# Local attention of a decoder: where the queries' reciprocal norms are applied, which engine guards them, and the order of the set-up

## The reference, cut to what matters

```python
q, k, v = split(h @ wqkv)                  # 8 heads of 64
q = q / max(norm(q), 1e-12) * q_scale
k = k / max(norm(k), 1e-12) * k_scale
q, k = rotary_xpos(q, k)                   # t * cos * s + rotate_half(t) * sin * s
sim = where(mask, -max, (q * 8) @ k.T)     # each window of 64 tokens and the one before
x = x + (softmax(sim) @ v) @ wo
```

## Time and profile before

| | |
|---|---|
| median of three runs | 3974.55 us |
| the profiled execution, its own time | 3975.32 us |
| its span in the profile | 3973.6 us |
| granted TensorE clock, mean | 0.986 |
| busy share of the span: TensorE, VectorE, ScalarE, GpSimd | 95%, 73%, 72%, 46% |
| layer 0 of local attention | about 1100 to 1640 us of the span |
| layer 1 | about 1801 to 2340 us |
| eight exponentials (L1168) | 312.0 us busy in 1024 operations, mean 389 ns |

### The profile page before, as it was taken

The page is one execution under the profiler, slowest core; times in us unless marked ns, Lnnn a source line. Parts: engine busy times, 40 slices in busy tenths (PEclk is TensorE's granted clock), DMA queues, the critical chain, the costliest instruction groups (busy, mean ns, idle before and its releaser), DMA issues. The chain is left out here.

```text
span 3973.6 us, 108219 instructions
## 1 busy us (share of the span) xinstructions
PE 3761.6 (95%) x35018; PEld 3030.0 (76%) x35018; DVE 2920.3 (73%) x7397; ACT 2875.6 (72%) x6740; POOL 1823.0 (46%) x1666
## 2 busy tenths in 40 slices
PE   8999899999979999897999989999999989998998
PEld 6777688888746666685666668788888877776888
DVE  7888655555579999656999965676777768886665
ACT  5555466656579999856999975677777768886665
POOL 5555322222268888635777764333333332111222
PEclk9999999999999999999999999999999999999999
DMA  1000100000100000100000010000000000000444
GB/s 30 19 20 19 53 7 7 6 6 6 41 11 8 8 8 8 24 22 9 9 8 8 9 25 20 17 0 0 0 0 0 0 1 4 3 4 25 126 121 116
DMA packets 130766, 80.29 MB, mean 20 GB/s; under 512 B 95328, under 2 KB 121184, under 8 KB 130016
## 3 DMA queue, kind: packets, MB, share of 16 engines
q1 hardware_dynamic: 130656, 78.87, 7.5%
HBM read 57.39 MB, written 4.72 MB: 16 GB/s over the span
## 5 line engine op out<-in xcount | busy, mean ns | idle before, releaser
L1101 POOL TENSOR_TENSOR l_rc<-l_rc,l_rs 128x1024 f32<-128x1024 f32 x128 | 303.6, 2372 | 201.8 <-DVE l_rs L1293 201.8
L1168 ACT ACTIVATE l_prob<-l_prob,l_mx 128x128 f32<-128x128 f32 x1024 | 312.0, 389 | 0.0
L672 POOL TENSOR_TENSOR ca_prob<-ca_prob,ca_sm 128x1232 f32<-128x1232 f32 x64 | 143.9, 2249 | 307.5 <-DVE ca_sm L835 307.5
L1779 POOL TENSOR_TENSOR mb_steps<-w_upto,mb_dta 128x1024 f32<-128x1024 f32 x64 | 121.4, 1897 | 345.8 <-DVE mb_dta L2047 345.8
L1193 PE MATMUL l_qk_ps<-w_local,l_hT 128*128 128x512 f32 x512 | 248.9, 610 | 12.5 <-DVE l_rs L1293 9.3
L1095 POOL TENSOR_TENSOR l_prob<-l_prob,l_sm 128x1024 f32<-128x1024 f32 x128 | 242.8, 1897 | 16.9 <-DVE l_sm L1279 16.9
L1078 POOL TENSOR_TENSOR l_rc<-l_rc,l_ss 128x1024 f32<-128x1024 f32 x128 | 243.4, 1902 | 12.4 <-POOL l_rc L1101 4.5
L1938 PE MATMUL mb_x_ps<-w_wx,mb_xT 128*128 128x256 f32 x1024 | 237.1, 385 | 0.0
L382 ACT ACTIVATE la_ef<-la_feat,la_fbias 128x1024 f32<-128x1024 f32 x128 | 135.6, 1110 | 122.2 <-PE la_feat L441 122.2
L346 POOL TENSOR_SCALAR la_ef<-la_ef,la_high,la_low 128x1024 f32<-128x1024 f32 x128 | 151.1, 1190 | 135.0 <-ACT la_ef L382 135.0
L1288 DVE TENSOR_REDUCE l_ss<-l_sq 128x16 f32<-128x1024 f32 x128 | 156.1, 1219 | 77.3 <-ACT l_sq L1132 76.5
(11 more groups left out here) (348 smaller groups left out, 11788.6 us busy)
## 6 DMA issues: line engine op xcount, KB each, us to landing
mo_spread<-parked SPq DMA_DIRECT2D x128, 256.0 KB
la_xin<-in_x SPq DMA_DIRECT2D x64, 64.0 KB
la_xT<-in_x_T SPq DMA_DIRECT2D x64, 64.0 KB, 1.8
l_h<-lt_y SPq DMA_DIRECT2D x128, 32.0 KB
lt_quad<-lt_y SPq DMA_DIRECT2D x32, 128.0 KB
out_x<-k_x SPq DMA_DIRECT2D x64, 64.0 KB, 1.6
l_h<-lt_y SPq DMA_DIRECT2D x128, 31.8 KB
lt_quad<-lt_y SPq DMA_DIRECT2D x32, 127.0 KB
```

The costliest lines, as they stand in the source:

```text
L1101: gp.tensor_tensor(wide(rc[l][:]), wide(rc[l][:]), wide(rs[l][:]), ALU.add).then_inc(*pool_sum.did("rot"))
L1168: ex = sc.activation(p[:, a, j], p[:, a, j], ACT.Exp, bias=mx[l][:, a, j:j + 1])
```

## The change

The norms of k are still applied to k, on GpSimd, but as a multiply of 512 elements. Those of q are no longer applied to q: they become the `scale` operand of the eight exponentials, one column of `ss` for each head, and the bias becomes the negated maximum times the reciprocal norm, `shift`, computed on GpSimd (128x8). `ss` has four buffers for that instead of two. The guard against zero is a maximum with 1e-24 on GpSimd instead of a Relu on ScalarE, and the Ln has no bias any more. The tables are laid out so that both sine products are one VectorE operation that doesn't swap halves; the swap moves into GpSimd's add, which becomes two operations of 512 elements, in runs of 32. TensorE's transposes of q wait for that add alone, those of k for the multiply. On ScalarE hT now comes ahead of the exponentials as before, then four exponentials, then Ln and Exp on `ss` (of batch n-3), then the other four. The quad rows are cleared after the other engines have been let go.

```diff
@@ set-up, semaphores
-        under, floor = m.sb("under", [128, 1]), m.sb("floor", [128, 1])
+        floor = m.sb("floor", [128, 2 * H])
-        ss = both(m, "ss", [T, 3, 2 * H])
+        ss = [m.sb(f"ss{i}", [T, 3, 2 * H]) for i in range(4)]
-        NZERO = 10
+        NZERO = 5
@@ sync
                 pipeline(sp, g.NB, OUT + 1, step, turn=4)
+                sp.wait_ge(cleared, 4)
@@ gpsimd
-                for slot in range(4):
-                    gp.memset(g.quads[slot][0:1], 0.0).then_inc(zeroed, 1)
-                gp.memset(under[:], -1e-24).then_inc(zeroed, 1)
-                gp.memset(floor[:], 1e-24 * 2.0 ** 20).then_inc(zeroed, 1)
+                gp.memset(floor[:], 1e-24).then_inc(zeroed, 1)
+                gp.wait_ge(zeroed, NZERO)
...
+                for slot in range(4):
+                    gp.memset(g.quads[slot][0:1], 0.0).then_inc(cleared, 1)
...
                     b = at(SCORE)
-                        gp.wait_ge(*pool_sum.at("rot", b))
                         gp.wait_ge(*act_rot.at("rn", b))
-                        gp.tensor_tensor(rc[l][:].rearrange("p a h e -> p (a h) e"), rc[l][:].rearrange("p a h e -> p (a h) e"),
-                                         ss[l][:, 2].unsqueeze(2).to_broadcast([T, 2 * H, HD]), ALU.mult
-                                         ).then_inc(*pool_norm.did("norm"))
+                        gp.wait_ge(*pool_sum.at("rot1", b))
+                        gp.tensor_tensor(rc[l][:, 1], rc[l][:, 1], ss[b.slot][:, 2, H:2 * H].unsqueeze(2).to_broadcast([T, H, HD]),
+                                         ALU.mult).then_inc(*pool_norm.did("norm"))
+                    b = at(SOFT)
+                        gp.wait_ge(*vec_max.at("max", b))
+                        gp.wait_ge(*act_exp.at("exp", b, ago=2))
+                        gp.tensor_tensor(shift[l][:], mx[l][:], ss[b.slot][:, 2, 0:H].rearrange("p (j a) -> p a j", a=2),
+                                         ALU.mult).then_inc(*pool_shift.did("shift"))
...
                     b = at(QKV)
-                        gp.wait_ge(*vec_rot.at("sin1", b))
-                        gp.tensor_tensor(wide(rc[l][:]), wide(rc[l][:]), wide(rs[l][:]), ALU.add
-                                         ).then_inc(*pool_sum.did("rot"))
+                        gp.wait_ge(*vec_rot.at("ss", b))
+                        gp.sem_inc(turns, 1)
+                        gp.tensor_scalar(ss[b.slot][:, 0], ss[b.slot][:, 0], floor[:, 0:1], None, ALU.max).then_inc(*pool_floor.did("ssm"))
+                        gp.wait_ge(*vec_rot.at("sin", b))
+                        for part, (lo, hi) in enumerate(((0, HD // 2), (HD // 2, 0))):
+                            out = rc[l][:].rearrange("p a h e -> p (a h) e")[:, :, lo:lo + HD // 2]
+                            other = rs[l][:].rearrange("p a h e -> p (a h) e")[:, :, hi:hi + HD // 2]
+                            gp.tensor_tensor(out, out, other, ALU.add).then_inc(*pool_sum.did(f"rot{part}"))
@@ scalar
-                    b = at(QKV)
-                        sc.wait_ge(*vec_rot.at("ss", b))
-                        sc.activation(ss[l][:, 0], ss[l][:, 0], ACT.Relu, bias=under[:]).then_inc(*act_rot.did("ssm"))
-                        sc.wait_ge(*act_rot.at("ssm", b))
-                        sc.activation(ss[l][:, 1], ss[l][:, 0], ACT.Ln, scale=2.0 ** 20, bias=floor[:]
...
                     b = at(SOFT)
-                        sc.wait_ge(*vec_max.at("max", b))
-                        for a in (0, 1):
-                            for j in range(PAIRS):
-                                ex = sc.activation(p[:, a, j], p[:, a, j], ACT.Exp, bias=mx[l][:, a, j:j + 1])
+                        sc.wait_ge(*pool_shift.at("shift", b))
+                        for j in range(PAIRS):
+                            sc.activation(p[:, 0, j], p[:, 0, j], ACT.Exp, bias=shift[l][:, 0, j:j + 1],
+                                          scale=ss[b.slot][:, 2, 2 * j:2 * j + 1])
+                    b = at(QKV)
+                        sc.wait_ge(*pool_floor.at("ssm", b))
+                        sc.activation(ss[b.slot][:, 1], ss[b.slot][:, 0], ACT.Ln, scale=2.0 ** 20).then_inc(*act_rot.did("lnn"))
+                        sc.wait_ge(*act_rot.at("lnn", b))
+                        sc.activation(ss[b.slot][:, 2], ss[b.slot][:, 1], ACT.Exp, scale=-0.5, bias=lnscale[:]
+                                      ).then_inc(*act_rot.did("rn"))
+                    b = at(SOFT)
+                        for j in range(PAIRS):
+                            ex = sc.activation(p[:, 1, j], p[:, 1, j], ACT.Exp, bias=shift[l][:, 1, j:j + 1],
+                                               scale=ss[b.slot][:, 2, 2 * j + 1:2 * j + 2])
                         ex.then_inc(*act_exp.did("exp"))
@@ tensor, SCORE
-                        te.wait_ge(*pool_norm.at("norm", b))
+                        te.wait_ge(*pool_sum.at("rot1", b))
                         for a, name in enumerate(("qT", "kT")):
+                            if a == 1:
+                                te.wait_ge(*pool_norm.at("norm", b))
@@ vector
                         v.wait_ge(*vec_max.at("mask", b))
+                        v.wait_ge(*pool_shift.at("shift", b, ago=2))
...
                         v.tensor_tensor(rc[l][:], qk, tab(0), ALU.mult).then_inc(*vec_rot.did("cos"))
-                        v.tensor_tensor(rs[l][:, :, :, lo], qk[:, :, :, hi], tab(1, lo), ALU.mult).then_inc(*vec_rot.did("sin0"))
-                        v.tensor_tensor(rs[l][:, :, :, hi], qk[:, :, :, lo], tab(1, hi), ALU.mult).then_inc(*vec_rot.did("sin1"))
+                        v.tensor_tensor(rs[l][:], qk, tab(1), ALU.mult).then_inc(*vec_rot.did("sin"))
```

More of the change, by code:

```diff
@@ L929, in laid_out @@
         scales = [d[f"L0_ffn_{side}_scale"][layer] for side in "qk"]
-        swapped = [np.roll(s, ROT_DIM // 2) for s in scales]
         local.append(packed("local", {
             "wqkv": d["L0_ffn_wqkv"][layer], "wo": chunks(d["L0_ffn_wo"][layer]),
-            "qks": np.concatenate([scales[0], swapped[0], scales[1], swapped[1]])}))
+            "qks": np.concatenate([scales[0], scales[0], scales[1], scales[1]])}))
         w2 = d["L0_ffn_w2"][layer]
@@ L999, in local_attention @@
         probT = both(m, "probT", [T, 2, PAIRS, T])
-        mx, sm = both(m, "mx", [T, 2, PAIRS]), both(m, "sm", [T, 2, H])
+        mx, shift, sm = both(m, "mx", [T, 2, PAIRS]), both(m, "shift", [T, 2, PAIRS]), both(m, "sm", [T, 2, H])
         attT = both(m, "attT", [2 * HD, PAIRS, T])
@@ L1005, in local_attention @@
         score_ps = m.ps("score_ps", [128, 2, PAIRS, T])
-        zeroed, prep = m.sem("zeroed"), m.sem("prep")
+        zeroed, cleared, prep, turns = (m.sem(n) for n in ("zeroed", "cleared", "prep", "turns"))
         h_in = m.lanes("h_in")
         vec_in = Stage(m.sem("vec_in"), "st0 mv0")
-        vec_rot = Stage(m.sem("vec_rot"), "ss cos sin0 sin1")
+        vec_rot = Stage(m.sem("vec_rot"), "ss cos sin")
         vec_max = Stage(m.sem("vec_max"), "mask max")
@@ L1024, in local_attention @@
         pe_att = Stage(m.sem("pe_att"), "pT0 pT1 pv ao")
-        pool_sum = Stage(m.sem("pool_sum"), "rot")
+        pool_sum = Stage(m.sem("pool_sum"), "rot0 rot1")
+        pool_shift = Stage(m.sem("pool_shift"), "shift")
+        pool_floor = Stage(m.sem("pool_floor"), "ssm")
         pool_norm = Stage(m.sem("pool_norm"), "norm")
@@ L1062, in _ @@
                 gp.memset(lnscale[:], 10.0 * float(np.log(2.0))).then_inc(zeroed, 1)
-                for slot in range(4):
-                    gp.memset(g.quads[slot][0:1], 0.0).then_inc(zeroed, 1)
                 for l in (0, 1):
                     gp.memset(h[l][:], 0.0).then_inc(zeroed, 1)
-                gp.memset(under[:], -1e-24).then_inc(zeroed, 1)
-                gp.memset(floor[:], 1e-24 * 2.0 ** 20).then_inc(zeroed, 1)
-                for stage in (pool_sum, pool_norm, pool_prob, pool_in):
+                gp.memset(floor[:], 1e-24).then_inc(zeroed, 1)
+                gp.wait_ge(zeroed, NZERO)
+                for stage in (pool_floor, pool_sum, pool_norm, pool_shift, pool_prob, pool_in):
                     stage.start(gp)
+                for slot in range(4):
+                    gp.memset(g.quads[slot][0:1], 0.0).then_inc(cleared, 1)
                 def step(at):
@@ L1146, in step @@
                         sc.activation(val[b.slot][:].rearrange("p h e -> p (h e)"), v_ps[:], ACT.Copy).then_inc(*act_v.did("v"))
-                    b = at(QKV)
-                    if b:
-                        l = b.lane
-                        sc.wait_ge(*vec_rot.at("ss", b))
-                        sc.activation(ss[l][:, 0], ss[l][:, 0], ACT.Relu, bias=under[:]).then_inc(*act_rot.did("ssm"))
-                        sc.wait_ge(*act_rot.at("ssm", b))
-                        sc.activation(ss[l][:, 1], ss[l][:, 0], ACT.Ln, scale=2.0 ** 20, bias=floor[:]
[L1154 to L1157, removed]
                     b = at(TURN)
@@ L1282, in step @@
```

(10 more changed lines are left out.)

12 lines of the change are left out of this document (9 added, 3 removed).

## The result

After the change four runs gave 4003.85 to 4005.51 us, median 4004.67; the kernel before gave 3976.49 beside it (3973.6 to 3978.43, four runs). The ratio is 1.0072 [1.0059, 1.0085]: 28 us slower, where +23 and 3998 us had been forecast (the forecast's sum gives 3998.3 for the profiled execution and, by its own 0.8 less, 3997.5 for the median). The profiled execution took 4003.85 us, its span is 4002.0. From the first memset of a stage to that of the next, layer 0 takes 565.4 us instead of 555.7 and layer 1 563.2 instead of 544.8, together +28.0. No other stage moves by more than 2 us.

The account below looks back on a forecast made before the run. Loop A was to bound both local attention layers at 8.32 us a batch; +28.1 steady, -2.8 fill and -2.3 start gave +23.0, so 3998 us for the median, range 3984 to 4014.

Parts of the forecast that it names:

- loop A: Local attention: ScalarE from copy of v to probT, then TensorE back to the next copy; 8.00 us, forecast 8.32.
- The pointer: Second per-partition pointer on the eight softmax exponentials: 0.092 us each, +0.74 us of ScalarE per batch.
- The low end of 0.056: Cheaper second pointer on the exponentials, +0.45 us a batch; as rival 3961 us, chance 0.06, plus 0.03 for no change.
- Relu and the Ln's pointer: Relu and the Ln's bias pointer leave ScalarE: -0.33 and -0.09 us per batch.
- Guard: The maximum on GpSimd, 128x16: taken as 0.2 us, at no cost on the path.
- Loop G: Two-batch loop through GpSimd's rotary add, norm multiply, transposes, ScalarE and VectorE: 16.40 us, forecast 15.4, no bound.
- k multiply: GpSimd's norm multiply cut from 1024 to 512 elements: 1.90 us to 1.04.
- halves: GpSimd's add as two operations of 512: 1.27 us each, +0.16 in all; slow-halves rival 4045 us, chance 0.07.
- The rival in which the pointer is free: Second pointer costs nothing; loop A 7.58, VectorE's 7.72 bounds layer 0, say 7.77; 3919 us, chance 0.06.
- fill: While each layer's pipeline fills, the shorter way over GpSimd stands open: -1.4 us per layer, -2.8.
- start: Quad rows cleared later: -1.8 us in layer 1, -0.5 in layer 0, together -2.3.
- the steady part: Pipeline filled in 61 of a layer's 72 steps, +0.15 us each in layer 0, +0.31 in layer 1: +28.1.

Follow-up runs that it names:

- Experiment 2: A per-partition scale pointer (a column of ones) added to the eight exponentials of the kernel before; 4062.16 us, ratio 1.0216.
- experiment 3: The changed kernel with immediate scale 1.0 in four of the eight exponentials of a batch; 3951.55 us, ratio 0.9943.
- experiment 1: The changed kernel with immediate scale 1.0 instead of the pointer in all eight exponentials; 3933.17 us, ratio to the kernel before 0.9892.
- experiment 5: The kernel of experiment 4 with Ln and Exp moved between the first and last four exponentials; 3973.45 us, ratio 0.9998.
- experiment 4: The kernel before with the guard alone moved to GpSimd, Ln without bias, Ln and Exp where they stood; 3991.49 us, ratio 1.0038.
- experiment 6: The changed kernel with one more GpSimd addition of 512 elements, into a spare buffer, ahead of the halves; 4009.04 us, ratio 1.0090.
- experiment 7: The changed kernel with the quad rows cleared ahead of the other engines' release again; 4000.06 us single, then 4001.23, changed kernel beside it 4003.52.
- run 1266: Not a follow-up run: a GpSimd addition of 512 elements lying in a single run takes 1266 or 1280 ns, seen in experiment 6.

## Why the prediction was right

**The direction and its cause** were right: loop A with eight second pointers sets the period in both layers. Experiment 2 gives the pointer's price in the old kernel, experiment 3 half of it in the new one, experiment 1 its absence.

**The pointer** was put at 0.092 us from rows of other stages and measured 0.091 (0.73/8) in experiment 2 and 0.093 (8.307 - 7.937, over four) in experiment 3. The low end of 0.056, from unlike sources, was the wrong reading. The Trainium skill, ScalarE: Activation LUTs, section What ACT_TABLE_LOAD costs, has 93 ns per pointer; these runs agree.

**Relu and the Ln's pointer.** ScalarE's stretch from v to probT grew from 3.88 to 4.18 us, +0.30 against the +0.32 worked out. The period measured 8.307 and 8.308 against 8.32.

**Guard.** Estimated at 0.2 us, it took 318 ns for 128x16, more than the shift's 204 ns; its eighth of the elements was no guide to its duration. In the change it is hidden all the same, by the order that experiment 5 isolates: with Ln ahead of all exponentials it costs some 17 us (experiment 4 against 5).

**Loop G.** k multiply 1042 ns (1.04), halves 1274 (1.27): as read from the earlier trace rows. In the after trace there is no batchwise wait of the transposes for GpSimd, and experiment 6 puts the loop at 15.54 (15.4).

**The rival in which the pointer is free** had the right sign and a wrong floor: 3919 us, against 3933 measured with immediate scales. It took VectorE's 7.72 us for the next bound; it was TensorE's own stream at 7.8. The rows were there: 392.84 of 400 us busy at 8.01 us is 7.87 a batch, an upper bound of that stream above both 7.58 and 7.77, which should have warned.

**The step that was mis-sized is the sum at the layers' ends.** With the copies of v as marks, layer by layer:

| us, after less before | layer 0 | layer 1 |
|---|---|---|
| first memset to the fourth copy of v | -1.67 | -3.73 |
| 59 further batches | +7.89 | +17.28 |
| the last distance of two copies of v | +1.81 | +1.73 |
| last copy of v to the next stage's first memset | +1.64 | +3.05 |
| sum | +9.67 | +18.33 |

The first line is 5.4 us gained, where "fill" and "start" had put -2.8 and -2.3. In layer 0 the start gave little: the release came earlier, but the clears then stood in front of GpSimd's own first subtraction (2.88 us behind the first memset, before 2.97). The second line is 25.2, the steady part. The forecast counted 61 distances in each layer, 28.1, so 2.9 more than that, and had no term for the drain, the stretch in which the last batches leave the pipeline. The drain is the last two lines, 8.2 us. In it:

- The last distance of two copies of v is longer by the steady 0.2 us a layer, 0.4, and by the lower clock of experiment 7, 1.6 in each layer, 3.2.
- Two batches in each layer go through eight exponentials after the last copy of v, with no Relu left to save: 4 x 0.74 = 3.0.
- A second stretch at the lower clock stands behind that copy in both layers. In layer 0 (product with wo 2.08 us instead of 1.16, the eight transposes of the probabilities 1.55 instead of 1.09, behind an idle time of 1.67 us) the exponentials cover it, and the stage ends only 0.2 us later than by them. In layer 1 it comes behind a later wait, of 2.00 us, with no exponentials beside it (2.00 instead of 1.16, 1.89 instead of 1.04) and takes some 1.6.

So nearly 5 us of the difference between +23 and +28 are time at a lower clock, which no step of the prediction had; the exponentials of the drain are about what the 2.9 too many in the steady part made up for. The range took "fill, drain and start" at 4 either way, so this part alone was off by a little more than that; the range held because the pointer came out where it had been put.

## What to carry to other kernels

A per-partition scale cost 0.09 us on each activation of 128x128, so a factor per row and head that costs one multiply elsewhere is dear when it becomes an operand of many small activations on the engine that closes the loop: here 8 x 0.09 us a batch for 1.9 - 1.04 us of GpSimd time, on a path that had held layer 0 back by no more than 0.16 us a batch (8.18 against 8.02) and layer 1 not at all. Before moving work, write down each loop across engines with its length, and the length of every engine's own stream as a floor; a change that relieves one loop is worth only the distance to the next. A small operation in another engine's queue is free only if what waits for it stands late enough in its own.

## What the runs showed of the hardware that had not been expected

- TensorE's clock fell to its lower level behind an idle time of 2.12 us in one program and not behind one of 2.11 us in another with the same instructions around it, where it fell one wait later, behind 1.67 us. In the kernel of experiment 3 it stayed up behind 1.75 us and fell after 1.30 us. So the length of the last idle time alone does not tell; the profile shows no difference that explains it. In the changed kernel its places were the same in both executions profiled, in the one with the clears first only in layer 0. What a fall costs depends on what runs beside it: some 1.6 us where TensorE was waited for, 0.3 us or less where eight exponentials covered it.
- GpSimd's tensor-scalar on 128x16 (318 ns) takes longer than its product of two tensors on 128x8 (204 ns).
- A GpSimd addition of 512 elements in runs of 32 takes 1274 ns, one in a single run 1266 or 1280 (experiment 6): the swap of halves inside the add costs nothing that can be measured.
